# Moving work of the third attention into the last steps of the second, and large loads from SyncE's queue to GpSimd's

## The reference

```python
x = layernorm(x + attn(x))                    # causal, 16 heads of 32, LoRA-merged weights, output projection
def xattn(x, ctx):
    h = mha(x, x, x)                          # second attention, biases, no mask
    x1 = ln(x + h)
    h = mha(x1, ctx, ctx)                     # third attention: 224 queries, 750 keys
    x2 = ln(x1 + h)
    return ln(x2 + relu(x2 @ fc1 + b1) @ fc2 + b2)
x = layernorm(x + xattn(x, ctx))
x = layernorm(x + bitlinear_ffn(x))           # rows quantized to 8 bits, weights to -1, 0, 1
```

## Time and profile before

| | |
|---|---|
| Median of 3 runs | 3251.22 us (3243.08 to 3252.54) |
| Profiled execution's own time | 3245.53 us |
| Its span, first to last instruction | 3243.7 us |
| Mean granted clock of TensorE | 0.978 |
| PE busy | 2988.8 us (92%), 34642 matmuls |
| DVE busy | 2567.3 us (79%) |
| ACT busy | 1995.7 us (62%) |
| POOL busy | 1349.9 us (42%) |

### The profile page before, as it was taken

One profiled execution on the slowest core, in us unless ns is written; L12 is line 12 of the kernel. 1 busy time (PEld: TensorE's weight loads), 2 busy tenths in 40 slices (PEclk: granted clock), 3 DMA queues, 4 the chain that ended last, 5 costly groups with the idle time before them and its releaser, 6 DMA issues.

```text
span 3243.7 us, 87025 instructions
## 1 busy us (share of the span) xinstructions
PE 2988.8 (92%) x34642; PEld 2369.2 (73%) x34642; DVE 2567.3 (79%) x4750; ACT 1995.7 (62%) x4650; POOL 1349.9 (42%) x1273
## 2 busy tenths in 40 slices
PE   7998999988999769999999999999889999999996
PEld 4987888888899647777877778877765565565662
DVE  4776888888899669999999999999846666666666
ACT  2655565667787537777777777877655445344352
POOL 0675632257765544444344344443132232222232
PEclk9999999999999889999999999999899999999997
DMA  4666655456554546655655555554341121211212
GB/s 127 185 206 223 194 180 153 135 159 202 174 162 140 150 118 134 141 141 125 140 137 134 137 135 147 134 129 106 125 152 40 46 53 53 56 45 44 56 40 49
DMA packets 430834, 405.86 MB, mean 125 GB/s; under 512 B 272368, under 2 KB 346240, under 8 KB 429280
## 3 DMA queue, kind: packets, MB, share of 16 engines
q1 hardware_dynamic: 415600, 348.64, 41.0%
q0 software_dynamic: 14576, 51.40, 5.1%
q10 hardware_dynamic: 256, 0.26, 0.0%
HBM read 239.98 MB, written 109.52 MB: 108 GB/s over the span
## 4 chain that ended last, share of the span: by engine, by line
PE 51%; DVE 18%; DMA 13%; ACT 8%; issue 4%; SPq 4%; POOL 1%; ACTq 0%; DVEq 0%; POOLq 0%
PE at_ps L769 22%; PE at_ps L1430 4%; PE at_ps L911 4%; PE at_ps L855 4%; DVE at_mx_cross L988 4%; DVE at_p L997 3%; DMA self_spill<-at_proj 3%; PE at_ps L1444 3%; PE at_ps L890 3%; PE at_ps L1455 3%; PE at_ps L1411 2%; ACT at_ps L945 2%; DVE at_proj L981 2%; DMA at_o_raw<-at_values 2%; PE at_ps L865 2%
## 5 line engine op out<-in xcount | busy, mean ns | idle before, releaser
L944 ACT ACTIVATE at_p<-at_ps 125x448 f16<-125x448 f32 (+2 forms) x1280 | 676.9, 529 | 285.9 <-PE at_ps L890 196.5
L997 DVE TENSOR_TENSOR at_p<-at_ps,at_p 125x448 f16<-125x448 f32 (+2 forms) x1280 | 750.5, 596 | 129.3 <-ACT at_ps L945 119.3
L945 ACT ACTIVATE at_ps<-at_ps 125x448 f32<-125x448 f32 (+2 forms) x1280 | 679.5, 531 | 0.0
L988 DVE TENSOR_REDUCE at_mx_cross<-at_ps 128x1 f32<-128x750 f32 x512 | 476.7, 931 | 26.9 <-PE at_ps L855 24.5
L1070 POOL TENSOR_TENSOR at_o_sum<-at_o_raw 128x256 f32<-128x256 f32 x192 | 121.2, 631 | 782.6 <-ACT at_o_raw L951 782.1
L911 PE MATMUL at_ps<-at_values,at_p 112*128 112x65 f16 (+3 forms) x6656 | 303.3, 185 | 23.4 <-DVE at_p L997 10.5
L1478 ACT ACTIVATE at_masks<-at_ps,at_b_cols 128x256 f32<-128x256 f32 x224 | 106.7, 476 | 336.2 <-PE at_ps L1411 336.1
L992 DVE TENSOR_REDUCE at_mx<-at_ps 112x2 f32<-112x448 f32 (+1 forms) x512 | 303.9, 609 | 10.0 <-PE at_ps L865 7.0
L1411 PE MATMUL at_ps<-at_xt,at_early 128*128 128x256 f16 x1792 | 302.1, 276 | 8.9 <-ACT at_w_first L1479 6.1
L911 PEld LDWEIGHTS at_ps<-at_values,at_p 112*128 112x128 f16 (+1 forms) x6656 | 267.2, 97 | 49.3 <-ACT at_o_raw L951 19.7
L1430 PE MATMUL at_ps<-at_w_second,at_w_first 128*128 128x512 f16 x896 | 283.6, 379 | 0.0
(11 more groups left out here) (217 smaller groups left out, 6941.7 us busy)
## 6 DMA issues: line engine op xcount, KB each, us to landing
at_x_res<-x SPq DMA_DIRECT2D x124, 256.0 KB, 3.2
cross_spill<-at_proj SPq DMA_DIRECT2D x64, 487.0 KB, 3.2
at_x_rows<-x SPq DMA_DIRECT2D x92, 256.0 KB, 3.1
at_prep<-bit POOLq DMA_DIRECT2D x32, 512.0 KB, 5.5
at_early<-ctx SPq DMA_DIRECT2D x32, 512.0 KB, 5.3
at_stacks<-cross_spill SPq DMA_DIRECT2D x64, 243.5 KB, 3.7
causal_spill<-at_proj SPq DMA_DIRECT2D x64, 224.0 KB, 3.5
at_stacks<-causal_spill SPq DMA_DIRECT2D x128, 112.0 KB, 2.3
```

Source lines behind the costliest of these rows:

```text
L944: act.activation(mem.p_hi[0:self.KC, n % 4, 0:self.P_COLS], scores, ACT.Exp, scale=EXP_SCALE)
L945: act.activation(scores, scores, ACT.Exp, scale=EXP_SCALE).then_inc(self.exp_done, 1)
L988: dve.tensor_reduce(self.mx[:, at, t, h:h + 1], mem.ps_qk[:, :, 0:self.KT // 2], AX.XY, ALU.max).then_inc(self.max_done, 1)
L997: dve.tensor_tensor(mem.p_lo[0:self.KC, n % 4, cols], mem.ps_st[0:self.KC, self.st_bank(b, g, n), cols], mem.p_hi[0:self.KC, n % 4, cols], ...
```

## The change

1. `change()`: steps 0 to 4 as before; then x0 and x1 of batch 0 behind step 5, c0 and c1 behind step 6, c2 to c5 in the first half of step 7. Unit 0 is spread over the second half of step 7 and step 8. Unit 1, with one maximum of unit 0 behind each piece, is spread over steps 9 to 11, and the splits of batch 1 stand ahead of steps 9, 10 and 11. Behind the last step come `row` of unit 0, x0 and x1 of batch 1, v's bias, the slots, the loads of batch 2, then unit 2 and c0 to c5 of batch 1 spread among the eight maxima of unit 1, and the first scores.
2. `load` and `load c` of the third attention, v's bias, gain and shift, and both loads of attention weights are issued by POOL instead of SP, with the same waits, at the same places of the list. The x rows get semaphores of their own.
3. The single-partition memset of groups 1, 2 and 3 becomes a DMA by POOL that copies group 0's row; the scores of these groups wait for it.

```diff
     def sync(self, sp, kind, b, g, n):
-        if kind == "load":
+        if kind == "load" and not self.cross:
...
-        elif kind == "load c":
...
     def tensor(self, pe, kind, b, g, n):
...
                 if self.cross and b == self.b0:
-                    pe.wait_ge(self.slots_set, 2 * g + 2)
+                    pe.wait_ge(self.slots_set, g + 2)
+                    if g > 0:
+                        pe.wait_ge(self.slots_in[g], 16)
...
     def gpsimd(self, pool, kind, b, g, n):
         mem, at = self.mem, b - self.b0
-        if kind == "split x":
-            pool.wait_ge(self.x_rows_in[b % 2], 32 * (b // 2 + 1))
+        if kind == "set slot" and g > 0 and n == 0:
+
+            pool.wait_ge(self.slots_set, 1)
+            if g == 1:
+                pool.wait_ge(self.proj_full, self.before.last_projected())
+            else:
+                pool.wait_ge(self.pv_done, self.before.pair_end)
+            pool.dma_start(self.ks(b, g)[96:97], self.ks(b, 0)[96:97]).then_inc(self.slots_in[g], 16)
+        elif kind == "load" and self.cross:
+            pool.wait_ge(self.stored, 32 * (b - self.NB + 1))
+            if self.back(b, 2).cross:
+                pool.wait_ge(self.x_split, b - 1 - self.b0)
+            else:
+                pool.wait_ge(self.proj_full, self.before.full_index["x1", b - 2, 0] + 1)
+            for t in range(2):
+                pool.dma_start(mem.x_rows[0:T // 2, b % 2, t, :], self.x_in[b - self.b0, t * T // 2:(t + 1) * T // 2, :]
+                               ).then_inc(self.cross_rows_in[b % 2], 16)
+        elif kind == "load c":
+            if b == self.b0:
+                pool.wait_ge(self.rows_clear, 1)
+            wait(pool, self.c_split, 3 * (b - self.b0 - 1) + n + 1 if b > self.b0 else 0)
...
+        elif kind == "weights in":
+
+            for n in range(2):
+                pool.dma_start(self.w_part[n], self.w[n].rearrange("p (c n) -> p c n", c=DC)).then_inc(self.w_in, 16)
...
         def change():
...
-            for events in steps[:7]:
+            inputs, ahead = cross.inputs(0), cross.inputs(1)
+            for events in steps[:5]:
                 yield from events
+            yield from steps[5] + inputs[0:2] + steps[6] + inputs[2:4]
             yield cross, "set slot", b0, 0, 1
             yield cross, "set slot", b0, 1, 0
             yield cross, "set slot", b0, 1, 1
-            rest = [e for events in steps[7:] for e in events] + [(own, "evacuate", b0 - 1, G - 1, 1)]
-            early = cross.inputs(0) + list(cross.unit(0)) + list(cross.unit(1))
-            yield from spread(early, rest)
+            half = len(steps[7]) // 2
+            yield from spread(inputs[4:], steps[7][:half])
+            yield from spread(list(cross.unit(0)), steps[7][half:] + steps[8])
+            yield cross, "split x", b0 + 1, 0, 0
+            second, maxima = list(cross.unit(1)), cross.maxima(0)
+            work = [e for n, event in enumerate(maxima) for e in
+                    second[n * len(second) // len(maxima):(n + 1) * len(second) // len(maxima)] + [event]]
+            yield from spread(work, [e for n in range(3) for e in [(cross, "split c", b0 + 1, 0, n)] + steps[9 + n]]
+                              + [(own, "evacuate", b0 - 1, G - 1, 1)])
+            yield cross, "row", b0, 0, 0
+            yield from ahead[0:2]
+            yield cross, "v bias in", b0, 0, 0
             for g in (2, 3):
                 for n in range(2):
                     yield cross, "set slot", b0, g, n
-            yield cross, "v bias in", b0, 0, 0
-            yield cross, "split x", b0 + 1, 0, 0
-            for n in range(3):
-                yield cross, "split c", b0 + 1, 0, n
             yield cross, "load", b0 + 2, 0, 0
             for n in range(3):
                 yield cross, "load c", b0 + 2, 0, n
-            work = list(cross.unit(2)) + cross.inputs(1)
-            yield from spread(work, [m for u in range(cross.MAX_AHEAD) for m in cross.maxima(u)])
-            yield cross, "row", b0, 0, 0
+            work = [e for n in range(6) for e in list(cross.unit(2))[2 * n:2 * n + 2] + ahead[2 + n:3 + n]]
+            yield from spread(work, [m for u in range(1, cross.MAX_AHEAD) for m in cross.maxima(u)])
             for n in range(cross.AHEAD):
                 yield cross, "scores", b0, 0, n
```

More of the change, by code:

```diff
@@ L231, in worked, with stored_through @@
         return self.done, self.number(k, ("split", "round")) + 1
-    def stored_through(self, sp, k):
+    def stored_through(self, pool, k):
         for place in range(2):
             last = max(j for j in range(k + 1) if j % 2 == place)
-            sp.wait_ge(self.stored[place], self.stores[place][last // 2] + 32)
+            pool.wait_ge(self.stored[place], self.stores[place][last // 2] + 32)
     def load(self, pool, m):
@@ L738, in sync @@
             sp.dma_start(self.x_out[b - self.b0, P:T, :], mem.y[2 * P - T:P, 1, :]).then_inc(self.stored, 16)
-        elif kind == "weights in":
-            for n in range(2):
-                sp.dma_start(self.w_part[n], self.w[n].rearrange("p (c n) -> p c n", c=DC)).then_inc(self.w_in, 16)
-        elif kind == "v bias in":
-            if before.norm is not None:
-                sp.wait_ge(self.res_done, before.NB)
-            sp.dma_start(mem.v_bias[:, :], self.biases[:, 2 * D:3 * D].partition_broadcast(P)).then_inc(self.v_bias_in, 16)
-        elif kind == "norm in":
-            if before.norm is not None:
-                sp.wait_ge(self.y_done, before.NB)
-            sp.dma_start(mem.gain[:, :], self.norm[0].partition_broadcast(P)).then_inc(self.gain_in, 16)
-            sp.dma_start(mem.shift[:, :], self.norm[1].partition_broadcast(P)).then_inc(self.gain_in, 16)
     def transposes(self, pe, bank, n, tiles):
@@ L1042, in gpsimd @@
         mem, at = self.mem, b - self.b0
-        if kind == "split x":
-            pool.wait_ge(self.x_rows_in[b % 2], 32 * (b // 2 + 1))
+        if kind == "set slot" and g > 0 and n == 0:
[18 more added lines that the diff above has]
+            wait(pool, self.c_split, 3 * (b - self.b0 - 1) + n + 1 if b > self.b0 else 0)
+            rows = self.kv_in[b - self.b0]
+            if n < 2:
+                two = rows[2 * n * P:(2 * n + 2) * P, :].rearrange("(c p) d -> p c d", p=P)
+                pool.dma_start(mem.c_rows[:, 2 * n:2 * n + 2, :], two).then_inc(self.c_rows_in[n], 16)
+            else:
+                for c in (4, 5):
+                    n_rows = min(P, self.KT - c * P)
+                    pool.dma_start(mem.c_rows[0:n_rows, c, :], rows[c * P:c * P + n_rows, :]).then_inc(self.c_rows_in[n], 16)
+        elif kind == "weights in":
+            for n in range(2):
+                pool.dma_start(self.w_part[n], self.w[n].rearrange("p (c n) -> p c n", c=DC)).then_inc(self.w_in, 16)
+        elif kind == "v bias in":
+            if self.before.norm is not None:
+                pool.wait_ge(self.res_done, self.before.NB)
+            pool.dma_start(mem.v_bias[:, :], self.biases[:, 2 * D:3 * D].partition_broadcast(P)).then_inc(self.v_bias_in, 16)
+        elif kind == "norm in":
+            if self.before.norm is not None:
+                pool.wait_ge(self.y_done, self.before.NB)
+            pool.dma_start(mem.gain[:, :], self.norm[0].partition_broadcast(P)).then_inc(self.gain_in, 16)
+            pool.dma_start(mem.shift[:, :], self.norm[1].partition_broadcast(P)).then_inc(self.gain_in, 16)
+        elif kind == "split x":
+            pool.wait_ge(self.cross_rows_in[b % 2], 32 * (at // 2 + 1))
@@ L1903, in _ @@
                     sp.dma_start(mem.b2_row[:, :], fc2_b.partition_broadcast(P)).then_inc(b2_in, 16)
-                elif kind == "second weights":
-                    preparation.stored_through(sp, 5)
-                    own.sync(sp, "weights in", own.b0, 0, 0)
-                elif kind == "third weights":
-                    preparation.stored_through(sp, 11)
-                    sp.wait_ge(causal.proj_free, causal.free_index["y1", NB - 1, 0] + 1)
-                    cross.sync(sp, "weights in", cross.b0, 0, 0)
             sp.wait_ge(signals.stored, 32 * NB * len(layers))
@@ L1981, in _ @@
                     preparation.gpsimd(pool, n)
+                elif kind == "second weights":
+                    preparation.stored_through(pool, 5)
+                    own.gpsimd(pool, "weights in", own.b0, 0, 0)
+                elif kind == "third weights":
+                    preparation.stored_through(pool, 11)
+                    pool.wait_ge(causal.proj_free, causal.free_index["y1", NB - 1, 0] + 1)
+                    cross.gpsimd(pool, "weights in", cross.b0, 0, 0)
 def decoder_layer(nc, x, ctx, attn, loras, sa, sa_bias, ln1, ca, ca_bias, ln2, fc1, fc1_b, fc2, fc2_b, ln3,
```

31 lines of the change are left out of this document (10 added, 21 removed).

## The result

The changed kernel takes 3254.82 us (median of 19 runs, 3241.28 to 3270.61), the kernel before 3245.24 us beside it (19 runs, 3239.78 to 3258.49): ratio 1.0026, 95% interval 1.0015 to 1.0037. The change costs a quarter of a per cent, where a gain of 46.7 us, 1.4 per cent, was forecast. The profiled execution has a span of 3251.3 us against 3243.7 before: +7.6.

A forecast was written before the change was run, and what follows sets the result against it. PE was taken to bound the kernel, DVE close behind. Terms -6 - 3.7 - 25 - 2 - 8 - 2 = -46.7 took the 3251.22 us median to 3204.5 us, range 3187 to 3231.

The forecast's parts named there:

- signs of being wrong: Steps 7 to 11 above 50 us; spill beside the weights still 16 us; POOL's sums delaying the steady batch.
- The hole: Between second and third attention: row ahead of transposes, memsets and eight maxima gone; 42.10 to 17 us, -25.
- Unit 2 is wanted only in the first step of the third attention, and a delay there is hidden by its 18 us: Stretch behind the hole: delay of unit 2 costs nothing; stretch goes from 22.32 to 20.3 us, -2.
- That wait goes: Steps 7 to 11: PE's 3.7 us wait for a context transpose vanishes through earlier inputs; 43 us, -3.7.
- Rival A: Steps 7 to 11: maxima and stack waits not covered, 61 us there and 3223 in all; chance 0.13.
- The spill's trouble is its queue: Steps 0 to 6: moving loads from SP to POOL and dropping a memset gives 54.8 us, -6.
- The second weights (-8): Second attention's 3 MB weight load on POOL's queue: spill no longer stands behind it; -8, bounds nothing to -12.2.
- The third weights (-2, bounds 0 to -4.9): Third attention's weight load on POOL's queue: costs less than the second's, gains 2 us.
- The steady third attention (0): Six loads per batch move to POOL without a new wait: 0, bounds +-5 us over the phase.
- rival C: Third attention: POOL becomes the late engine, its issues delaying fifteen steady batches, 68 us at full price, 3272; chance 0.05.
- B: Large loads gain nothing by their queue, the 16 engines being the limit: steps 0 to 6 -0.8, weights 0, 3220; chance 0.12.
- D: First scores still wait for the row behind SP, so the hole keeps 11 us of transposes: 3215; chance 0.08.

The follow-up runs named there:

- e4: Changed kernel with all loads (both attention weights, vectors, third attention's x and context) back on SP, new order kept: 3242.41 us, ratio 0.9967.
- f2: e4 with batch 1's last six transposes and batch 2's loads moved behind unit 2, its stack and the first scores: ratio 0.995.
- h1: f1 and f2 combined, second attention's weights and vectors on POOL, first unit's k and v from mid step 8 to mid step 9: 3223.38 us, ratio 0.9926.
- e2: Changed kernel with only the third attention's x and context loads back on SP, at the same places of the order: 3245.84 us, ratio 0.9987.
- f3: Changed kernel, loads still on POOL, with the order of f2: ratio 0.9987.
- g3: f1 and f2 combined, second weights and vectors on POOL, batch 0's transposes one step earlier, k and v back in step 7: ratio 0.9937.
- f1: e4 with only q of the first unit in step 7's second half and its other nine pieces in step 8: ratio 0.9961.

## Why the prediction was wrong

From steps 0 to the first reciprocal of the third attention the kernel before takes 172.0 us, the changed one 170.1, e4 161.5, f2 153.2, h1 151.1; forecast was 172.0 - 36.7 = 135.3. The largest steps that failed are the stretch behind the hole, steps 7 to 11 and the third weights. Of the prediction's own signs of being wrong the first came (steps 7 to 11 above 50: 56.0), the second nearly (the spill beside the weights 15.0 us, for 16), the third did not.

**The hole (-25): right,** by its own reasons: 18.1 for 17, PE busy 15.31 for 14.3. The row is ahead of the transposes and nothing but unit 2 and eight maxima is left.

**"Unit 2 is wanted only in the first step of the third attention, and a delay there is hidden by its 18 us": this step failed, with 15.8 us** (36.1 for 20.3). The first maximum of that step stands near its front, in PE's order, and everything behind it waits: 13.14 us. I had seen that the transposes share SP with the spill, 1.3 us each by the earlier trace rows, and gave the delay no price; beside POOL's loads two took 10.33. Two causes, told apart: the transposes and loads ahead of the stack (e4 to f2: 6.0 us in hole and stretch together) and the loads on a second queue (changed kernel to e2: 9.5 us). Together they are 15.5 of the 16.9 by which hole and stretch exceed their forecast (54.2 for 37.3). That they fit so well is in part luck: by the means of all kernels the queue's part is 6.6 us (51.3 to 44.7), or 7.3 with the late order (47.0 in f3, 39.7 as the mean of the five others), and the order's 5.0 (44.7 to 39.7).

**"That wait goes" (steps 7 to 11, -3.7): failed, +9.3.** I counted the four inputs that move ahead and not the four that stay; k needs all six context transposes, and even the two of them that moved ahead still ran in step 7. SP's pace, some 1.3 us each between stores and stacks, puts the last one at 1120.66, 10.3 us into step 7, and naming more of them earlier does not bring it forward (13.2 us into step 7 in g3); the first k had been moved in front of it. f1 and h1 put k back and recover 4.6 and 5.2 us in steps 7 and 8, less what the later steps take. Rival A, which had these steps at 61 for the maxima and their stacks, comes nearer in size than the forecast and has the wrong cause: all waits for cross maxima and their stack in them are 3.9 us. Even in h1 the five steps stay at 56.1, of which PE is busy 39.45 at a clock of 0.85 (33.5 at full clock, near my 34.7): 43 was too little for the latencies between.

**"The spill's trouble is its queue" (steps 0 to 6, -6): failed in steps 0 to 4, -0.9 in all.** Of the 12 us above a steady pace 8.2 lie in steps 0 to 4 (43.0 for 5/4 of 27.86), and there the spill's queue did not set the time: relief of SP does speed up steps 0 to 3 (32.3 to 28.6), but z by POOL ends step 4, and my sum had POOL's issues in the steady third attention and nowhere the 3.97 us of them in front of z. Steps 5 and 6 fell by 4.9 (17.8 to 12.9; 11.2 to 16.6 in the twelve experiments), as they should without the memset of the earlier trace rows, though no run has that edit alone. With the loads on SP steps 0 to 6 are 54.6 to 59.6 us (median 56.5 of eight kernels), with them on POOL 57.6 to 59.9.

**The second weights (-8): right in sign, about half in size.** -3.2 in this profile; over nine kernels with these weights on POOL batches 6 and 7 are 74.4 to 78.4 us, over five with them on SP 79.8 to 85.4, means 76.8 and 81.3: -4.5. "The spill no longer stands behind them" was true of the queue and not of the time: 15.0 us for 16.7. The Trainium skill (DMA: Bandwidth & Descriptors, Queues, rings and completion order) says that each engine takes the queues in turn, one packet at a time; from that the prediction had the spill wait for about its own volume. The trace agrees with the page and not with my use of it. From 297 to 305 us POOL's queue moved 319 packets and SP's 321, one for one, but with 2.84 MB against 0.23: 8.9 KB a packet against 0.7 (548 and 347 packets from 305 to 312 us). So SP's queue, with the spill in it, got a twelfth of POOL's volume, and the spill took 15.0 us, where the median landing of such a spill is 3.1 on the page of the profile. No run here varied the packet size.

**The third weights (-2, bounds 0 to -4.9): wrong in sign, +8.6.** "Cost less" took the queue for the only thing that changes, and left out who issues first. On SP the weights stood behind the stack that PE wants next; POOL issues them 0.3 us ahead of it. That this order is the cause is read from the two timelines; no run put POOL's issue behind the stack. That the queue costs here is shown: batches 18 and 19 take 72.9 to 76.8 us in five kernels with them on POOL, 65.8 to 72.2 in eight others with them on SP (before itself 67.9): means 75.3 and 68.3 (with before).

**The steady third attention (0): right.** Fourteen batches take 1038.4 us before, 1040.4 after, and 1040.2 to 1043.4 in the twelve experiments; rival C is out. DVE in a two-port mode starving POOL's loads of descriptors, of which the Trainium skill (SBUF — State Buffer, SBUF: two separate sides) warns, shows no cost here either: the changed kernel's batch is 74.90 us with DVE busy 67.63. Whether DVE was in such a mode meanwhile no run shows.

**Rivals B and D:** B's worst case was that the new queue gains nothing; that it could lose had no price anywhere in my sum but rival C's. The loss came because a load on its own queue is also a load that nobody holds back, and because POOL's issues stood in front of z. D is out, the row was in time.

The misses are 15.8 + 13.0 + 5.1 + 4.8 + 10.6 + 1.0 (the hole) = 50.3; with the 4.1 outside these stages they are the distance from -46.7 to +7.6, but for rounding.

## What to carry to other kernels

A queue that issues in order is also a brake: a large load behind a stack on the same queue waits for it, and on an idle engine's queue it goes out early and meets the small transfers that PE is waiting for. Before moving loads to another engine, look at which small DMA is due while the load is under way (here 13.5 to 16.1 us) and whether the load should go behind it, and price the new engine's whole order in each stage, not only where it is busiest. When work is moved forward, list everything its first instruction needs and find when the slowest of these is done: here the sixth context transpose set the time, and an instruction put in front of it on an in-order engine stopped work that was ready.

## What the runs showed of the hardware

- DMA transposes slow down beside foreign traffic and hold the issuing engine meanwhile: two held SP 2.63 us at 1170.94 and 10.33 us at 1177.36 in the same kernel, the latter beside loads on POOL's queue, which moved 2.7 MB from 1165 to 1205 us. With the loads on SP itself and ahead of them, two took 6.58 us (e4). Ordinary DMAs are held too: the two stack DMAs behind the 10.33 us took 4.08 us to issue, where such a pair took 0.81 before.
- Two queues with work shared the engines packet for packet and not byte for byte: 319 and 321 packets, 2.84 and 0.23 MB, from 297 to 305 us of the changed kernel.
- POOL needs 0.54 to 0.82 us to issue one large DMA, in its order, and the context loads so issued beside other traffic landed in 13.5 to 16.1 us (SP's, in f2: 5.8).
- PE's granted clock was at the 1.2 GHz level (0.50) in 732 to 737, 1118 to 1123 and 1192 to 1202 us of the changed kernel; in the 5 us ahead of each PE was busy 0.61, 0.02 and 0.62 us. Behind the first it was 0.69 in the next 5 us and 1.00 in the 5 after those.
